# Issuing the four transfers of wx3 from ScalarE's queue instead of SyncE's, in a four-layer conditioned kernel

## The reference

```
x = x + (x * ys) @ W0 * d                      # ys, d from the condition
x = x + scan: h = tanh(h @ Wh1 + x_t @ Wx1 + b1)            # plain recurrence, 128 steps
x = x + (x + x @ (base + A_b B_b^T))           # A_b, B_b of rank 8, from gelu(LN(cond) @ w1 + b1) @ w2
x = x + scan: LSTM(x_t @ Wx3 + h @ Wh3 + b3)                # 512 x 2048 weights, 128 steps
```

## Time and profile before

| what | us |
|---|---|
| median of 3 runs | 1130.18 (1129.91 to 1130.26) |
| own time of the profiled execution | 1131.51 |
| span of the profiled execution | 1129.7 |
| PE busy | 1092.5 (97%) |
| DVE busy | 885.4 (78%) |
| ACT busy | 426.1 (38%) |
| POOL busy | 16.7 (1%) |

### The profile page before, as it was taken

One profiled execution on the slowest core, in us unless ns is written; L12 is line 12 of the kernel. 1 busy time (PEld: TensorE's weight loads), 2 busy tenths in 40 slices (PEclk: granted clock), 3 DMA queues, 4 the chain that ended last, 5 costly groups with the idle time before them and its releaser, 6 DMA issues.

```text
span 1129.7 us, 65707 instructions
## 1 busy us (share of the span) xinstructions
PE 1092.5 (97%) x30300; PEld 741.5 (66%) x30300; DVE 885.4 (78%) x2786; ACT 426.1 (38%) x1034; POOL 16.7 (1%) x48
## 2 busy tenths in 40 slices
PE   5779999999999999999999999999999999999997
PEld 3436666676766667676766767666766766676657
DVE  7888878777787877778777777887777778777765
ACT  5884333333333333333333333333333333333322
POOL 1000000000000000000000000000000000000000
PEclk9989999999999999999999999999999999999999
DMA  9991000000000000000000000000000000000000
GB/s 337 404 379 40 23 23 3 22 23 23 22 22 23 6 20 22 23 22 22 23 9 16 23 23 22 23 23 14 12 23 22 23 22 22 13 4 13 13 13 22
DMA packets 24644, 51.96 MB, mean 46 GB/s; under 512 B 4160, under 2 KB 4288, under 8 KB 23344
## 3 DMA queue, kind: packets, MB, share of 16 engines
q1 hardware_dynamic: 23936, 47.49, 11.9%
q10 hardware_dynamic: 432, 0.26, 0.1%
HBM read 39.36 MB, written 8.39 MB: 42 GB/s over the span
## 4 chain that ended last, share of the span: by engine, by line
PE 91%; DMA 4%; DVE 3%; issue 1%; ACT 1%; ACTq 0%; DVEq 0%
PE ps_gates L1563 57%; PE ps_l L1502 8%; PE ps_x L1502 7%; PE ps_l L1615 7%; PE ps_rnn L1615 7%; DMA ring<-in_hw 3%; PE ps_lr L1502 2%; PE ps_z L1532 1%; PE ps_l L1563 1%; DVE big L840 1%; DMA rows<-in_ln_b 1%; PE ps_gates L1471 1%; DVE gates_ring L1126 0%; PE ps_l L1449 0%; DVE b_lo L840 0%
## 5 line engine op out<-in xcount | busy, mean ns | idle before, releaser
L1563 PE MATMUL ps_gates<-big,rows 128*32 128x512 f16 (+1 forms) x6144 | 358.5, 376 | 1.2 <-ACT rows L525 1.2
L1563 PE MATMUL ps_gates<-big,lstm_h 128*32 128x512 f16 (+1 forms) x6144 | 348.9, 376 | 1.0 <-DVE lstm_h L1159 1.0
L1563 PEld LDWEIGHTS ps_gates<-big,lstm_h 128*32 128x32 f16 x6144 | 163.9, 97 | 156.2 <-DVE lstm_h L1159 2.4
L1563 PEld LDWEIGHTS ps_gates<-big,rows 128*32 128x32 f16 x6144 | 161.9, 97 | 141.1 <-issue 1.3
L1126 DVE SCALAR_TENSOR_TENSOR gates_ring<-ps_gates,tile_un,rows 128x256 f32<-128x256 f32 x252 | 110.6, 480 | 94.2 <-PE ps_gates L1563 94.2
L666 ACT ACTIVATE gates_ring<-gates_ring 128x256 f32<-128x256 f32 x128 | 53.4, 417 | 257.6 <-DVE gates_ring L1126 257.6
L1502 PE MATMUL ps_l<-xs,w_hi 128*128 128x128 f16 x1024 | 80.2, 222 | 0.8 <-issue 0.6
L1502 PE MATMUL ps_x<-x,base_hi 128*128 128x128 f16 x1024 | 78.1, 219 | 0.0
L525 ACT ACTIVATE xs<-xsT,tile_s 128x512 f16<-128x512 f32 x32 | 23.1, 721 | 114.6 <-DVE xsT L853 111.1
L1502 PEld LDWEIGHTS ps_l<-xs,w_hi 128*128 128x128 f16 x1024 | 63.1, 100 | 3.1 <-issue 1.6
L1502 PEld LDWEIGHTS ps_x<-x,base_hi 128*128 128x128 f16 x1024 | 62.5, 98 | 1.4 <-issue 1.4
(11 more groups left out here) (221 smaller groups left out, 1710.9 us busy)
## 6 DMA issues: line engine op xcount, KB each, us to landing
ring<-in_hw SPq DMA_DIRECT2D x16, 1024.0 KB, 14.7
xT_sb<-in_xT SPq DMA_DIRECT2D x32, 256.0 KB, 2.8
outT<-late SPq DMA_DIRECT2D x32, 256.0 KB, 2.0
big<-in_wx SPq DMA_DIRECT2D x5, 1024.0 KB, 14.6
big<-in_wh SPq DMA_DIRECT2D x5, 1024.0 KB, 14.3
big<-in_w SPq DMA_DIRECT2D x1, 1024.0 KB, 5.8
big<-in_hw SPq DMA_DIRECT2D x1, 1024.0 KB, 13.4
late<-in_base SPq DMA_DIRECT2D x1, 1024.0 KB, 14.3
```

Of the source, the lines that this page charges most:

```text
L1563: last = nc.tensor.matmul(by_chunk_of_gate(bank[B * j:B * j + B, columns]), of_step, tile_columns(w, j)[:, gates], start=start, stop=stop, ...
```

## The change

The four transfers leave SP's list, where they stood behind `b1T`, and are issued by ACT through its own queue, after its wait for `w0` and ahead of its squares of w0. The buffers, the semaphores they raise and every computing instruction stay the same.

```diff
@@ -423,8 +423,6 @@
             for c in range(1, XT_RING - 1):
                 load_x(c)
             sp.dma_start(b1T_sb[:], b1T).then_inc(ld_b1, 16)
-            for k in range(KC):
-                sp.dma_start(wx3_staged(k), by_row(wx3)[:, k]).then_inc(ld_wx3[k], 16)
             for n in range(RING, 2 * RING):
                 sp.wait_ge(w2_used, n - RING + 1)
                 load_w2(n)
@@ -688,6 +686,8 @@
             act.wait_ge(consts_ready, 1)
             nc.scalar.activation(unused[:], cell[:, 0:1], ACT.Sqrt)
             act.wait_ge(ld_w0, 16)
+            for k in range(KC):
+                act.dma_start(wx3_staged(k), by_row(wx3)[:, k]).then_inc(ld_wx3[k], 16)
             squares(big[:, SQ_SLOT], big[:, W0_SLOT], 1)
             act.wait_ge(ln_var_ready, 1)
             nc.scalar.activation(ln_s[:, 1:2], ln_s[:, 0:1], ACT.Sqrt).then_inc(ln_root_ready, 1)
```

## The result

The changed kernel takes 1137.97 us (median of 6 runs, 1134.83 to 1138.53) against 1130.22 of the kernel before in the same series: ratio 1.0063, 95% interval 1.005 to 1.0076. It is slower by 7.75 us. The forecast was 1135.9 with a range to 1141.8. In a second series, on another occasion, the same kernel took 1136.23 (1135.10 to 1137.53, 5 runs) against 1130.28: ratio 1.0054, interval 1.004 to 1.0068. The forecast's own range, 1133.5 to 1138, holds the first result by 0.03 us. The profiled execution before was 1.3 us slower than its median, so the two profiled spans differ by less than the medians: 1136.2 - 1129.7 = 6.5 us.

The account below looks back on a forecast made before the run. The prologue to 93.5 us was taken as bound by full DMA engines and DVE side by side. +9.96 moved, -1.9 slack, -0.6, -0.96, -0.92 regained gave +5.6 to +5.7: 1135.9 us, own range 1133.5 to 1138, full range 1131.6 to 1141.8.

Parts of the forecast that it names:

- from 93.5 us to the end nothing that the change touches runs: After PE's first gates product at 93.55 us: this stretch keeps its length; the change only moves its start.
- 9.96 us moved ahead, hw1 at 26.7: DMA queue: wx3's 4 MB, 9.96 us of all engines, pass SP's queued transfers; hw1 lands at 26.7 instead of 16.7.
- Less slack, +8.1 at DVE: Early prologue: hw1's lateness less 1.9 us slack; DVE takes PE's next product at 31.3 instead of 23.18, +8.1.
- tile 1 of x a second floor: Prologue, DVE: tile 1 lands at 38.7 instead of 28.8, wanted at 30.90; an independent floor of +7.9 us.
- ACT's four issues at nothing: Ahead of ACT's squares of w0: up to 4.3 us of issuing, priced at nothing because ACT then waits for late wx1.
- The three idle times regained: DVE in the prologue: waits of 0.86 (wx3 maximum), 0.96 (base landing) and 0.92 us (PE) fall away.
- DMA engines never run dry: Prologue transfers: the engines stay supplied, SP's old queue lasting to 39.4 us, so base lands at 53.8 as before.
- The sum: Whole prologue: +9.96 moved, -1.9 slack, -0.6, -0.96 and -0.92 regained, giving +5.6 to +5.7 us.
- Held by SP: Rival, chance 0.22: ACT's fourth issue is held by SP's issue until 20.7 us; +11.6 instead of +9.1, time 1138.4.
- Slow mixing of two queues: Rival, chance 0.10: two busy queues move fewer bytes, hw1 and x come 3 to 5 us later still; 1139 to 1141.
- Little effect: Rival, chance 0.11: ACT's queue gets only an eighth of the engines' time, wx3 hardly earlier; +0.6, 1130.8.
- faster: Rival, chance 0.07: wx3 fills leftovers, SP's first transfers keep their times, DVE loses three idle times; -2.7, 1127.5.

Follow-up runs that it names:

- e5: Against the kernel before: ACT issues all four wx3 transfers through its own queue, but late, behind gelu; 1132.29 us, ratio 1.0016.
- e3: Against the kernel before: wx3 stays on SP's queue, moved up behind hw1 and the small bias, ahead of hw2's pieces; 1135.99 us, ratio 1.006.
- e4: Against the kernel before: wx3 on SP's queue behind hw1, x tiles 1 and 2 and b1T, ahead of hw2's pieces 0 to 3; 1136.24 us, ratio 1.0061.
- after_again: The changed kernel, unaltered, timed again in a second series against the kernel before; 1136.23 us, ratio 1.0054.
- e8: Against the kernel before: ACT issues the four wx3 transfers behind its squares of wx1, while SP's own issues are held; 1138.41 us, ratio 1.0068.

## Why the prediction was right

*What bounds it.* The step "from 93.5 us to the end nothing that the change touches runs" holds: the part behind the first gates product is 1136.2 - 100.84 = 1035.4 us long, against 1129.7 - 93.55 = 1036.2 before. Over all profiles this part lies between 1034.2 and 1036.2 us; I have not looked for the cause of that spread, and it is as large as some differences of single profiles.

*9.96 us moved ahead, hw1 at 26.7.* Right to 0.1 us (26.7, read at 26.78). The share that I worked out for wx3, 65%, was too low; it is 79%. The sum did not hang on it, but the estimate of e5 did.

*Less slack, +8.1 at DVE; tile 1 of x a second floor.* Right (+8.25). e3 shows the second floor in DVE's wait of 8.49 us, with the pieces late as well. The third, pieces 0 to 3 of hw2, was missing from the text; e4 shows it. It changed nothing here: in the changed kernel PE takes the pieces at 37.34 without a wait.

*ACT's four issues at nothing.* Right by luck, for another reason than the one given. I had wx1 land up to 10 us late as their cover. It was not late: ACT read it at 11.18 without a wait. The cover was ACT's own idle time around the root, 1.72 and 0.61 us.

*The three idle times regained.* Right, all three gone. "DMA engines never run dry" was wrong: near 39 us they all but stopped for about 1 us, until piece 4, issued at 38.5, got going. It cost nothing, as DVE was the bound by then.

*The sum.* +5.6 to +5.7 forecast; 98.98 - 93.55 = +5.4 in the profile of after_again, +7.3 in the first. The missing term is the half clock at the end of the prologue, +1.6 us in some executions. It comes with PE's longer wait there (2.31 us, 0.96 before), which the lateness of the other engines brought. The medians, +7.75 and +5.95, lie 2.0 and 0.3 us above the forecast. That the first still lay in the stated range owes something to luck: the upper part of that range was meant for held issues and slow mixing, not for the clock.

*The rivals.* Held by SP: refuted by e8. Slow mixing of two queues: refuted, 416 GB/s while both were busy. Little effect, and faster: refuted by the landing times.

## What to carry to other kernels

When the DMA engines are full, a second queue is not more bandwidth but a change of order, and here the queue with the larger packets took the larger part of the engines. Before a transfer is moved forward, list all that it passes, with each one's landing and the time at which its first reader wants it: the change costs the largest lateness less the slack behind it, and repairing one of several level floors brings nothing. A busy chain regains lateness only in its own idle times, so a small move is free and a large one is paid for the rest. A transfer that comes late also makes PE wait, and PE may then run its next products at half clock: in e3 and e4 this came to about 1 us on top of the lateness.

## What the runs showed of the hardware that was not expected

- Two queues took turns packet by packet, 407 to 404 packets in 9 us, whatever their size: 8 KB packets got 79% of the time against 2 KB packets. The same transfers mixed at 416 GB/s, against 387 for 2 KB packets alone.
- An issuing instruction of ACT was not held by SP's issue that stood for 9 us beside it, and it ran while ACT was still busy with a computing instruction (both at 11.46 and 11.47 us in e8).
- A wait of PE of 2.3 us at the end of the prologue was followed by a stretch of half clock in three profiles (changed, e3, e8) and not in a fourth (e4), at a price of 1.6 us on the critical chain; with 1.9 us of products in the wait the five runs lay within 0.8 us.
- Behind waits of PE for late transfers or for DVE, half clock lasted 6 to 15 us (granted 0.50: e3 from 30 to 45, e4 from 33 to 42, e5 from 36 to 42), and products with one piece of hw2 took 1.94 us instead of 0.91.
